# The first group of outputs moved up behind the last group of scores, in a fused perceiver kernel on one core

## The chip, the cores and the metric

The kernel runs on one core of one Trainium2 chip. The metric is the device time of one execution in microseconds. A core has five engines that run side by side: TensorE (matrix products, PE in the profile), VectorE (DVE), ScalarE (ACT), GpSimd (POOL) and SyncE (SP), whose queue issues transfers here. They wait for one another by semaphores, and each engine works through its own list of instructions in the order written.

## The reference

The input x is (4, 256, 256): four batches, 256 tokens, 256 features; a context is (4, 4096, 256). Three parts are added to x one after another: a masked cross attention to the context, a linear attention, and a stack of six layers of local attention and feed-forward. The change lies in the third part:

```python
def local_attention(q, k, v):      # 16 heads of 64, windows of 64 tokens
    sim = jnp.einsum('bhwie,bhwje->bhwij', bq, bk2) * QK_SCALE
    sim = jnp.where(mask, -jnp.finfo(sim.dtype).max, sim)
    attn = jax.nn.softmax(sim, -1)
    out = jnp.einsum('bhwij,bhwje->bhwie', attn, bv2)

def attn_layer(x, Wqkv, qs, ksc, Wo):
    qkv = x @ Wqkv                  # 256 -> 3 * 1024
    q = l2norm(q) * qs              # and k; then a rotation with a scale
    out = local_attention(q, k, v)
    return out @ Wo

for i in range(6):
    x = attn_layer(shift_tokens(x), ...) + x
    x = ffn_layer(shift_tokens(x), ...) + x
```

A token attends to the tokens of its own window of 64 and of the one before. `shift_tokens` takes half of the features from the token before.

## The kernel before

The kernel runs four stages in turn; only the third, `local_layers` (line 1363 on), is of interest here. Its order of work is written out by hand, one function per engine, and the order within each engine is fixed by the calls.

**Slots.** The stage works in slots, one batch of one layer each: 6 layers of 4 batches are 24 slots. In a slot, TensorE (`slot`, line 1659) does the attention of batch b, the projections to queries, keys and values of the next batch (`ahead`; not in the very last slot), and the feed-forward of the batch before (`ffn`; not in the first). Layers 1 to 4 are a loop on each engine; layers 0 and 5 stand outside it. The input of the batch two slots on is turned as well (`turn`).

**TensorE's units.** `turn_qk` turns queries and keys (16 heads, in 8 groups through PSUM). `scores(a, g)` computes the scores of 4 heads (two pairs) as 32 matmuls in tiles of 64 by 64. `turn_probs(a, pair)` turns the probabilities of one pair with 4 matmuls into the one bank TURN. `out(a, L, b, g)` multiplies the turned probabilities of two pairs with the values, as 24 matmuls in tiles of 128 by 64, into the bank OUT. `project(n, nb, j)`, j from 0 to 11, is one unit of 6 matmuls with 512 columns, for a split of each number into a high and a low part; units 0 to 7 give queries and keys, 8 to 11 values. They alternate between two banks, so unit j waits until unit j - 2 has been copied out. `turn_xn`, `widen` (six) and `narrow` are the feed-forward, `project_out` the attention's last product.

**What stands around them.** ScalarE (`slot`, line 1821) copies each projection out (`qkv_out`, line 1765), takes the exponentials of a pair (`exps`, four instructions, line 1786), copies turned probabilities out (`probs_out`, line 1793) and some outputs (`o_out`, line 1800). Its order around the change is: exps 4, exps 5, qkv_out 7, qkv_out 8, probs_out 2, exps 6, qkv_out 9, o_out 0, qkv_out 10, probs_out 3, qkv_out 11, and then xn_out. The buffer `pT` has two halves, so probs_out 2 overwrites what the first group of outputs reads, and waits for it; the conditions are in these lines:

```python
def probs_out(a, pair):
    act.wait_ge(o_full, a + 4 * (pair // 2))
    act.wait_ge(pT_full, a + 2 * pair + 2)
def out(a, L, b, g):
    pe.wait_ge(pT_done, a + 4 * (g + 1))
    pe.wait_ge(o_done, a + 4 * g)
```

VectorE (`slot`, line 2106) adds the band mask, scales and takes the minima of a pair (`minima`, line 2023), divides by the totals (`share`, line 2039), rotates and normalises queries and keys, and does the gated products of the feed-forward (`gated`, line 2089).

**Weights.** In the third slot of each layer (b = 2) but the last layer, SyncE's queue loads the next layer's query and key weights (`load_layer_weights`, line 180) as four transfers of 512 KB. It waits for the eighth projection, unit 7, of that slot:

```python
sp.wait_ge(qkv_full, L + U * 3 + 8)
k.load_layer_weights(sp, i + 1, "qk")
```

ScalarE rounds them in twelve pieces (`weights_high`, line 1754) through that slot. The first piece stands right behind `xn_out` and ahead of probs_out 4, the input's copy (`x_out`), exps 7, probs_out 5, the second piece and the first gate (`gates`, line 1818). The queue's next entries are the values' small transfers (`middle`, lines 1479 and 1480), which wait for the last projection.

Of the kernel before, what the change touches and what calls it, by code (L numbers as in the profile page):

```python
# [116 lines left out]
def hold(eng, sem):  # L117

    eng.sem_inc(sem, 1)
# [1243 lines left out]
def local_layers(k):  # L1363
# [8 lines left out]
    with ExitStack() as ctx:  # L1372
# [48 lines left out]
        def score_at(pair, e, t):  # L1421

            bank, col = (2 if pair // 2 % 2 else 4) + e, (pair % 2) * T + t * P
            return bank, slice(col, col + P)
# [90 lines left out]
        def _(pe):  # L1515
# [10 lines left out]
            def project(a, b, j):  # L1526

                if j == 0:
                    pe.wait_ge(xT_done, a + U)
                    pe.wait_ge(u_done, a - 2 * U)  # L1530
                if b == 0 and (j < 4 or j in (8, 9)):
                    pe.wait_ge(w_low, a + after_piece(2 * (j if j < 4 else j - 4) + 1))
                t, part = divmod(j, 4) if j < 8 else divmod(j - 8, 2)
                col = part * 512 if j < 8 else 2 * INNER + part * 512
                if j >= 2:
                    pe.wait_ge(qkv_done, a + j - 1)
                for kk in range(KD):
                    for n, (px, pw) in enumerate(PARTS):
                        ins = pe.matmul(ps[:, DENSE + j % 2, :], xT[:, px, kk, t * P:(t + 1) * P], wqkv[pw][:, kk, col:col + 512],  # L1539
                                        start=kk == 0 and n == 0, stop=kk == KD - 1 and n == 2)  # L1540
                ins.then_inc(qkv_full, 1 if j < SLOTS - 1 else U - SLOTS + 1)

            def turn_qk(a):
                pe.wait_ge(rope_done, a + U)
                pe.wait_ge(q_rope_done, a + U)
                pe.wait_ge(s_read, a)
                for g in range(8):
                    two, s = divmod(g, 2)
                    if g == 2:
                        pe.wait_ge(y_mid, a)  # L1550
                    if g == 3:
                        pe.wait_ge(y_out, a - U + LAYER)
                    if g >= 4:
                        pe.wait_ge(k_done if s else q_done, a + 4 * (two - 1))
                    for i in range(2):
                        for t in range(TT):
                            col = s * INNER + (2 * two + i) * P
                            ins = pe.transpose(ps[:, TURN_QK[g % 4], i * T + t * P:i * T + (t + 1) * P],  # L1558
                                               qk[:, t, col:col + P], k.ident)
                    ins.then_inc(qk_full, 2)  # L1560

            def scores(a, g):

                if g < 2:
                    pe.wait_ge(q_done, a + 4 * (g + 3))
                    pe.wait_ge(k_done, a + 4 * (g + 3))
                else:
                    pe.wait_ge(s_read, a + 4 * (g - 1))
                hold(pe, pe_held)
                for pair in (2 * g, 2 * g + 1):  # L1570
                    for t in range(TT):
                        for n in range(2):
                            w = 2 * t + n
                            k0 = max(w - 1, 0) * WINDOW
                            for e in range(2):
                                head = slice(e * DH, (e + 1) * DH)
                                bank, cols = score_at(pair, e, t)
                                ins = pe.matmul(ps[n * WINDOW:(n + 1) * WINDOW, bank, cols],  # L1578
                                                qT[head, pair, w * WINDOW:(w + 1) * WINDOW], kT[head, pair, k0:k0 + P],
                                                start=True, stop=True)  # L1580
                ins.then_inc(s_full, 4)

            def turn_probs(a, pair):
                pe.wait_ge(p_done, a + 2 * pair + 2)
                pe.wait_ge(pT_done, a + 2 * pair)
                for i in range(2):
                    for t in range(TT):
                        at = (i * TT + t) * P
                        ins = pe.transpose(ps[:, TURN, at:at + P], prob[:, 2 * (pair % RING) + i, t, :], k.ident)  # L1589
                ins.then_inc(pT_full, 2)  # L1590
# [5 lines that stand above are left out]
                if g == 0:  # L1596
                    pe.wait_ge(qkv_done, a + U)
                    pe.wait_ge(mid_in[b % 2], L + 32 * (b // 2 + 1))
                for pair in (2 * g, 2 * g + 1):
                    at = (pair % 2) * T  # L1600
                    for values, t, q0, q1 in ((v[:, b % 2, 0, :], 0, 0, P), (v_mid[:, b % 2, :], 1, 0, WINDOW),
                                              (v[:, b % 2, 1, :], 1, WINDOW, P)):
                        for i in range(2):
                            col = (2 * pair + i) * DH
                            ins = pe.matmul(ps[i * DH:(i + 1) * DH, OUT, at + t * P + q0:at + t * P + q1],  # L1605
                                            values[:, col:col + DH], pT[:, pair % 2, i, t, q0:q1], start=True, stop=True)
                ins.then_inc(o_full, 4)
# [12 lines left out]
            def turn_xn(a, ahead):  # L1620
                pe.wait_ge(xn_done, a + U)
                if ahead:
                    pe.wait_ge(qkv_done, a + 2 * U + SLOTS - 1)
                pe.wait_ge(u_done, a)
                for kk in range(KD):
                    for t in range(TT):
                        ins = pe.transpose(ps[:, DENSE, kk * T + t * P:kk * T + (t + 1) * P],  # L1627
                                           xn[:, t, kk * P:(kk + 1) * P], k.ident)
                ins.then_inc(xnT_full, U)
# [29 lines left out]
            def slot(L, b, ffn, ahead, turn):  # L1659

                a = L + U * b
                f, fb = L + U * (b - 1), (b - 1) % B
                n, nb = L + U * (b + 1), (b + 1) % B
                turn_qk(a)
                scores(a, 0)
                if ahead:
                    project(n, nb, 0)
                scores(a, 1)
                if ahead:
                    project(n, nb, 1)  # L1670
                    project(n, nb, 2)
                turn_probs(a, 0)
                if ahead:
                    project(n, nb, 3)
                    project(n, nb, 4)
                scores(a, 2)
                turn_probs(a, 1)
                if ahead:
                    project(n, nb, 5)
                    project(n, nb, 6)  # L1680
                scores(a, 3)
                turn_probs(a, 2)
                if ahead:
                    project(n, nb, 7)
                    project(n, nb, 8)
                out(a, L, b, 0)
                if ahead:
                    project(n, nb, 9)
                    project(n, nb, 10)
                turn_probs(a, 3)  # L1690
                if ahead:
                    project(n, nb, 11)
                if ffn:
                    turn_xn(f, ahead)
                out(a, L, b, 1)
                turn_probs(a, 4)
                if turn:
                    turn_x(L + U * (b + 2), (b + 2) % B)
                if ffn:
                    widen(f, fb, 0, turn)  # L1700
                turn_probs(a, 5)
                if ffn:
                    widen(f, fb, 1, turn)
                out(a, L, b, 2)
                turn_probs(a, 6)
                if ffn:
                    widen(f, fb, 2, turn)
                turn_probs(a, 7)
                if ffn:
                    widen(f, fb, 3, turn)  # L1710
                out(a, L, b, 3)
                if ffn:
                    widen(f, fb, 4, turn)
                    widen(f, fb, 5, turn)
                project_out(a, b)
                if ffn:
                    narrow(f, fb)
# [640 lines left out]
```

## Time and profile before

| | |
|---|---|
| device time, median of 3 runs | 2299.36 us (2296.36 to 2299.97) |
| the profiled execution's own time | 2297.52 us |
| its span | 2295.7 us |
| TensorE matmul busy | 2117.8 us, 92% of the span, 16354 instructions |
| VectorE busy | 1706.1 us, 74% |
| ScalarE busy | 1337.3 us, 58% |
| GpSimd busy | 494.0 us, 22% |
| mean granted clock of TensorE | 0.971 of full speed |
| chain that ended last, by engine | PE 54%, issue 2%, ACT 2%, DVE 1%, DMA 1% |

The local stage runs from about 907 us to the end. The span is from the first to the last instruction that the profiler records. In a row of the timeline the columns are start, duration (both in us), engine, line of the kernel, operation, output and inputs, shapes and a count; in brackets stands how long the engine was idle before it and what ended that. Matmuls overlap, so the time of a unit is read from its start to the start of the next.

### The profile page before, as it was taken

Reading aid. Unit: us, or ns where it says so; the run is one execution under the profiler, and the core shown is the slowest. Engines: PE = TensorE matmul, PEld = TensorE weight load, DVE = VectorE, ACT = ScalarE, POOL = GpSimd, SP = SyncE. Lnnn points to the kernel's source line nnn. Section 1 sums busy time; section 2 is a strip of 40 time slices with the busy share of each in tenths; the row PEclk is TensorE's granted clock in tenths of the full one; section 3 lists DMA queues with packets and bytes.
Section 4 is the critical chain, followed back from the end, with each engine's and each line's share of the span. In section 5 each row is a group of like instructions: output and inputs, shape, how many; then the busy total and the mean of one; then the engine's idle time right before and its main releaser. Section 6 shows DMA issues by size and latency. Waiting matters only on the chain.

```text
span 2295.7 us, 49701 instructions
## 1 busy us (share of the span) xinstructions
PE 2117.8 (92%) x16354; PEld 1715.7 (75%) x16354; DVE 1706.1 (74%) x4834; ACT 1337.3 (58%) x3908; POOL 494.0 (22%) x274
## 2 busy tenths in 40 slices
PE   3899999999998665899999999999999999999986
PEld 3677777777776444788888888888888888888875
DVE  5777577567564466789888978897889788988872
ACT  1667556556554004567666766676667666766651
POOL 2111111111110002223222322232223222322210
PEclk9999999999999787899999999999999999999998
DMA  3000000000000400002110211021102110111000
GB/s 112 7 10 1 6 11 1 6 11 1 6 24 1 147 0 10 13 13 68 31 49 13 68 33 49 13 68 33 49 13 67 33 49 18 62 31 49 13 13 21
DMA packets 47107, 70.12 MB, mean 31 GB/s; under 512 B 9078, under 2 KB 33828, under 8 KB 46628
## 3 DMA queue, kind: packets, MB, share of 16 engines
q1 hardware_dynamic: 44516, 62.34, 8.8%
q10 hardware_dynamic: 2368, 4.98, 0.6%
q8 instruction: 119, 1.95, 0.3%
q14 instruction: 104, 0.85, 0.1%
HBM read 50.54 MB, written 1.05 MB: 22 GB/s over the span
## 4 chain that ended last, share of the span: by engine, by line
PE 54%; issue 2%; ACT 2%; DVE 1%; DMA 1%; POOL 0%; SPq 0%; DVEq 0%; ACTq 0%; POOLq 0%
PE ps_loc L1539 17%; PE ps_loc L1645 10%; PE ps_loc L1616 7%; PE ps_loc L1655 5%; PE ps_loc L1578 4%; PE ps_loc L1589 4%; PE ps_loc L1605 4%; PE ps_loc L1558 3%; DMA late<-y_all 1%; ACT prob_loc L1786 0%; PE ps_loc L1627 0%; DMA w_raw<-in_ffn_Wqkv_dram 0%; PE ps_loc L1522 0%; ACT L1818 0%; POOL rnorm L2269 0%
## 5 line engine op out<-in xcount | busy, mean ns | idle before, releaser
L2269 POOL TENSOR_TENSOR rnorm<-norm_floor,half_loc 128x32 f32<-128x32 f32 x48 | 302.4, 6300 | 621.2 <-DVE norm_floor L1959 499.1
L1539 PE MATMUL ps_loc<-w_high,xT 128*128 128x512 f32 x1152 | 379.1, 410 | 5.4 <-DVE w_low L1948 3.8
L1786 ACT ACTIVATE prob_loc<-prob_loc,top_loc 128x128 f32<-128x128 f32 x768 | 298.5, 398 | 40.1 <-DVE top_loc L2023 37.3
L1645 PE MATMUL ps_loc<-xnT_loc,w 128*128 128x256 f32 (+1 forms) x1056 | 252.7, 385 | 2.4 <-DVE kT_loc L2089 1.2
L644 ACT ACTIVATE prob<-prob,new_top 128x256 f32<-128x256 f32 x512 | 252.1, 496 | 0.0
L1539 PEld LDWEIGHTS ps_loc<-w_high,xT 128*128 128x128 f32 x1152 | 204.7, 189 | 55.7 <-issue 11.8
L820 DVE CUSTOM_DVE_ANT_0 prob<-ps_cross,bias 128x256 f32<-128x256 f32 x512 | 186.2, 420 | 71.2 <-PE ps_cross L435 57.6
L2023 DVE CUSTOM_DVE_ANT_0 prob_loc<-ps_loc,const,rnorm 128x128 f32<-128x128 f32 x768 | 218.6, 344 | 27.2 <-PE ps_loc L1578 25.5
L1778 ACT ACTIVATE qT_loc<-ps_loc 128x512 f32<-128x512 f32 x96 | 57.3, 597 | 301.2 <-PE ps_loc L1558 301.2
L1539 PE MATMUL ps_loc<-w_low,xT 128*128 128x512 f32 x576 | 228.4, 397 | 0.0
L1645 PEld LDWEIGHTS ps_loc<-xnT_loc,w 128*128 128x128 f32 (+1 forms) x1056 | 191.4, 190 | 28.9 <-DVE kT_loc L2089 2.4
L1616 PE MATMUL ps_loc<-wo,qT_loc 128*128 128x256 f32 x768 | 171.8, 382 | 0.8 <-ACT qT_loc L1800 0.8
L1616 PEld LDWEIGHTS ps_loc<-wo,qT_loc 128*128 128x128 f32 x768 | 147.3, 192 | 21.8 <-issue 1.0
L1015 POOL TENSOR_TENSOR o<-o,alpha 128x1024 f32<-128x1024 f32 x32 | 60.9, 1904 | 455.2 <-DVE o L859 350.7
L1786 ACT ACTIVATION_READ_ACCUMULATOR prob_loc<-prob_loc,top_loc 128x1 f32 x768 | 150.4, 196 | 0.0
L458 PE MATMUL ps_cross<-const,prob 128*128 128x128 f32 x1024 | 141.5, 282 | 6.7 <-ACT probT L652 4.0
L458 PEld LDWEIGHTS ps_cross<-const,prob 128*128 128x128 f32 x1024 | 111.0, 141 | 45.8 <-issue 30.6
L1793 ACT ACTIVATE pT<-ps_loc 128x512 f32<-128x512 f32 x192 | 113.9, 593 | 49.6 <-PE ps_loc L1589 37.8
L2039 DVE TENSOR_TENSOR prob_loc<-prob_loc,total_loc 128x512 f32<-128x512 f32 x192 | 132.5, 690 | 2.7
L435 PE MATMUL ps_cross<-kT,qT 64*128 64x256 f32 x1024 | 129.3, 391 | 5.5 <-DVE chunk_top L820 4.2
L1589 PE MATMUL ps_loc<-const,prob_loc 128*128 128x128 f32 x768 | 122.3, 282 | 10.5 <-DVE prob_loc L2039 8.1
L1655 PE MATMUL ps_loc<-w,kT_loc 128*128 128x256 f32 x576 | 128.3, 379 | 1.2 <-DVE kT_loc L2089 1.2
(184 smaller groups left out, 4265.8 us busy)
## 6 DMA issues: line engine op xcount, KB each, us to landing
w_raw<-in_ffn_Wqkv_dram SPq DMA_DIRECT2D x24, 512.0 KB, 5.4
v_mid<-v_loc SPq DMA_DIRECT2D x48, 256.0 KB, 3.6
w_raw<-in_ffn_Wqkv_dram SPq DMA_DIRECT2D x24, 256.0 KB, 4.0
wo<-in_ffn_Wo_dram SPq DMA_DIRECT2D x24, 256.0 KB, 3.6
w<-in_ffn_W_dram SPq DMA_DIRECT2D x12, 341.0 KB, 3.9
w<-in_ffn_W_dram SPq DMA_DIRECT2D x6, 640.0 KB, 4.8
ctx_raw<-in_ctx_dram SPq DMA_DIRECT2D x12, 256.0 KB, 2.6
w<-in_ffn_W_dram SPq DMA_DIRECT2D x12, 256.0 KB
```

Of the source, the lines that this page charges most:

```text
L458: ins = pe.transpose(ps[:, TURN + t, (i * TT + lt) * P:(i * TT + lt + 1) * P], prob[:, lt, 2 * pair + i, t * P:(t + 1) * P], k.ident)
L644: ins = act.activation(prob[:, t, h, :], prob[:, t, h, :], ACT.Exp, bias=new_top[:, t, h:h + 1], scale=-1.0, accum_out=chunk_sum[:, t, h:h ...
L820: ins = dve.tensor_tensor_reduce(out=prob[:, t, h, :], in0=ps[:, banks[pair % 2] + i, t * CHUNK:(t + 1) * CHUNK], in1=key_bias, scale=1.0, ...
L1539: ins = pe.matmul(ps[:, DENSE + j % 2, :], xT[:, px, kk, t * P:(t + 1) * P], wqkv[pw][:, kk, col:col + 512], start=kk == 0 and n == 0, sto ...
L1589: ins = pe.transpose(ps[:, TURN, at:at + P], prob[:, 2 * (pair % RING) + i, t, :], k.ident)
L1616: ins = pe.matmul(ps[:, WIDE_OUT, t * D:(t + 1) * D], oT[:, pair, t * P:(t + 1) * P], wo[:, pair, :], start=pair == 0, stop=pair == PAIRS - 1)
L1645: ins = pe.matmul(ps[0:n, DENSE + m % 2, part * T:(part + 1) * T], w1[:, kk, col:col + n], xnT[:, kk, :], start=kk == 0, stop=kk == KD - 1)
L1655: ins = pe.matmul(ps[:, FFN_OUT, t * D:(t + 1) * D], uT[:, m, t * P:(t + 1) * P], w2[:, m, :], start=m == 0, stop=m == FM - 1)
L1786: ins = act.activation(pr, pr, ACT.Exp, bias=top[:, h, t:t + 1], scale=-1.0, accum_out=total[:, h, t:t + 1])
L2023: ins = dve.tensor_tensor_reduce(out=prob[:, 2 * (pair % RING) + e, t, :], in0=ps[:, bank, cols], in1=band, scale=rnorm[:, b % 2, t, h:h + ...
L2039: dve.tensor_tensor(pr, pr, by, ALU.mult).then_inc(p_done, 2)
L2269: pool.tensor_tensor(rnorm[:, b % 2, t, :], norm2_floor[:, :], half[:, :], ALU.pow).then_inc(rnorm_done, 8)
```

## The change

The call of the first group of outputs, `out(a, L, b, 0)`, moves on TensorE from behind the projections 7 and 8 to directly behind the last group of scores, ahead of `turn_probs(a, 2)` and of these two projections. The four projections 7 to 10 then follow one another. No other engine's order is touched.

```diff
@@ -1679,12 +1679,11 @@
                     project(n, nb, 5)
                     project(n, nb, 6)
                 scores(a, 3)
+                out(a, L, b, 0)
                 turn_probs(a, 2)
                 if ahead:
                     project(n, nb, 7)
                     project(n, nb, 8)
-                out(a, L, b, 0)
-                if ahead:
                     project(n, nb, 9)
                     project(n, nb, 10)
                 turn_probs(a, 3)
```

## Rows read from the trace of the kernel before

**Rows 1.** Busy time in one slot: stretch and length, then each engine (instructions), clock, DMA.

```profile
1132.23:1188.30 56.07, 56.05 (x469) 46.83 (x468) 46.45 (x123) 36.75 (x104) 14.84 (x4) 1.00 0.11 32
```

**Rows 2.** Timeline of that slot, TensorE, from the last scores on.

```profile
1150.23 1.10 PE L1578 MATMUL ps_loc<-kT_loc,qT_loc 64*64 64x128 f32 x32
1151.27 0.66 PE L1589 MATMUL ps_loc<-const,prob_loc 128*128 128x128 f32 x4
1151.68 0.71 PE L1539 MATMUL ps_loc<-w_high,xT 128*128 128x512 f32 x2
...
1153.16 0.63 PE L1539 MATMUL ps_loc<-w_high,xT 128*128 128x512 f32 x2
...
1154.65 0.44 PE L1605 MATMUL ps_loc<-pT,v_loc 128*64 128x128 f32 x4
...
1155.71 0.73 PE L1539 MATMUL ps_loc<-w_high,xT 128*128 128x512 f32 x2
...
1157.21 0.63 PE L1539 MATMUL ps_loc<-w_high,xT 128*128 128x512 f32 x2
...
1158.61 0.60 PE L1589 MATMUL ps_loc<-const,prob_loc 128*128 128x128 f32 x4
1158.96 0.71 PE L1539 MATMUL ps_loc<-w_high,xT 128*128 128x512 f32 x2
...
1160.44 0.60 PE L1627 MATMUL ps_loc<-const,xn_loc 128*128 128x128 f32 x4
```

**Rows 3.** Timeline of the same stretch, ScalarE.

```profile
1154.76 0.60 ACT L1765 ACTIVATE v_loc<-ps_loc 128x512 f32<-128x512 f32 x1
1155.87 0.60 ACT L1793 ACTIVATE pT<-ps_loc 128x512 f32<-128x512 f32 x1 [0.51 <-PE ps_loc L1605]
1156.59 0.40 ACT L1786 ACTIVATE prob_loc<-prob_loc,top_loc 128x128 f32<-128x128 f32 x1
...
1158.15 0.58 ACT L1765 ACTIVATE v_loc<-ps_loc 128x512 f32<-128x512 f32 x1
...
1160.70 0.60 ACT L1765 ACTIVATE v_loc<-ps_loc 128x512 f32<-128x512 f32 x1 [0.52 <-PE ps_loc L1539]
1161.19 1.02 ACT L1809 ACTIVATE xnT_loc<-ps_loc,vec 128x256 f32<-128x256 f32 x2
```

**Rows 4.** The same stretch, VectorE: the last step of the pair's minima.

```profile
1156.21 0.34 DVE L2023 CUSTOM_DVE_ANT_0 prob_loc<-ps_loc,const,rnorm 128x128 f32<-128x128 f32 x1
```

**Rows 5.** Timeline of the third slot, ScalarE.

```profile
1043.41 0.41 ACT L1786 ACTIVATE prob_loc<-prob_loc,top_loc 128x128 f32<-128x128 f32 x1 [0.34 <-DVE top_loc L2023]
...
1044.97 0.58 ACT L1765 ACTIVATE v_loc<-ps_loc 128x512 f32<-128x512 f32 x1
```

**Rows 6.** Timeline of the third slot, TensorE.

```profile
1045.60 0.73 PE L1539 MATMUL ps_loc<-w_high,xT 128*128 128x512 f32 x2
...
1047.12 0.38 PE L1627 MATMUL ps_loc<-const,xn_loc 128*128 128x128 f32 x2
```

**Rows 7.** The chain that ended last, third slot: start, length, what.

```profile
1041.31 7.68 DMA w_raw<-in_ffn_Wqkv_dram
...
1049.01 0.41 ACT w_high L1754
```

**Rows 8.** The weight load of slot 7: durations in ns, first and last start.

```profile
L180 SPq DMA_DIRECT2D w_raw<-in_ffn_Wqkv_dram x4: 333/336/356, 1265.8 to 1267.4; - x4
...
DMA to landing us min/median/max: 3.9/5.1/6.2
```

**Rows 9.** Timeline of slot 7, ScalarE: its first weight rounding.

```profile
1274.33 0.64 ACT L1754 ACTIVATE w_high<-w_raw 128x512 fp32r<-128x512 f32 x1
```

**Rows 10.** Timeline of the last slot, TensorE: the turns of pairs 2 and 3.

```profile
2225.77 0.66 PE L1589 MATMUL ps_loc<-const,prob_loc 128*128 128x128 f32 x4 [1.58 <-DVE prob_loc L2039]
...
2228.67 0.63 PE L1589 MATMUL ps_loc<-const,prob_loc 128*128 128x128 f32 x4 [1.20 <-ACT pT L1793]
```

**Rows 11.** Waits from 906 to 2209 us: who, for what, us in total, times, longest.

```profile
ACT qT_loc L1778 <- PE ps_loc L1558: 288.3, 92, 12.4
```

## The prediction

> **What bounds the kernel now.** I began with the busy time of one slot of the local stage. A slot is one batch of one layer; there are 24, and 23 of them also carry the projections of the next batch. In the slot of [rows 1] TensorE is busy 56.05 of 56.07 us, at full clock, so only its own work and its rare waits count there. The page's chain agrees: it runs over TensorE nearly everywhere. Next I read TensorE in order of time through the part that is edited [rows 2], then ScalarE over the same stretch [rows 3] and the one VectorE step that gates it [rows 4]. I use these names for the units of work: S3 is the last scores, O0 the first outputs, T2 and T3 are turns of probabilities, P7 to P11 projections, N the turn of the normalised input. [Rows 2] give S3 at 1150.23, T2 1151.27, P7 1151.68, P8 1153.16, O0 1154.65, P9 1155.71, P10 1157.21, T3 1158.61, P11 1158.96, N 1160.44: no idle. S3 to N is 10.21 us, and the other 22 slots with projections repeat it within 0.1.
>
> ScalarE is less loaded but comes close. Its copy of P9 starts at 1158.15 and lasts 0.58, so it ends at 1158.73 [rows 3]; P11 cannot start without it and starts at 1158.96. The margin is 0.23 us. In the third slot there is none: there the copy of P9 starts at 1044.97 and ends at 1045.55 [rows 5], and P11 starts at 1045.60 [rows 6], 0.05 after it.
>
> **The change, part by part.** Nothing is added or taken away in work; O0 goes ahead of T2, P7 and P8. Four things follow.
>
> (1) **TensorE's own time shrinks.** From [rows 2]: S3 lasts 1.04, O0 1.06, T2 behind a group in small tiles 0.41, the projection behind a turn 1.48, one between projections 1.40 (P10 to T3), T3 0.35. P8 takes 1.49 because O0 follows, P9 takes 1.50 because O0 is ahead of it. The new order would run O0 1151.27, T2 1152.33, P7 1152.74, P8 1154.22, P9 1155.62, P10 1157.02, T3 1158.42, P11 1158.77 at the earliest: 0.19 sooner. The one junction that no row shows is S3 to O0. S3 has 1.04 ahead of T2, and I take the same ahead of O0. Its bounds: no cheaper, since S3's matmuls are the same; at most 0.10 dearer, which is what P8 pays ahead of O0 (1.49 against 1.40).
> The Trainium skill (TensorEngine Tiling (Array Packing), Key Properties) says that a change of tiling mode drains the engine. By that rule the stretch has four changes now and three afterwards, and leaving S3 costs the same whatever follows. The extra 0.09 and 0.10 in P8 and P9 agree with it; taken alone, the rule would promise the 0.19 in every slot.
>
> (2) **ScalarE takes it back.** Its order is fixed: copy of P8, probabilities out of T2 (p2), four exponentials (e6), copy of P9. Now p2 waits for O0, because it overwrites the buffer that O0 reads: the row at 1155.87 has 0.51 of idle put down to O0, and the copy of P8 was done during O0, from 1154.76 [rows 3]. With O0 early, that wait is gone, but P8 ends where O0 ended, and its copy now stands ahead of p2. A copy after a long wait starts 0.26 after the next unit's start (N 1160.44 in [rows 2], copy 1160.70 in [rows 3]); after a short one about 0.20 (0.11 behind O0's start, plus the 0.09 by which P8 is lengthened). So the copy starts at 1155.82 to 1155.88, p2 0.49 later (1160.70 to 1161.19), e6 0.47 to 0.49 after that: 1156.78 to 1156.86, in place of 1156.59. Until now e6 waited for the minima, whose last step runs from 1156.21 for 0.34 [rows 4]; this cover is what is used up. In the third slot e6 starts at 1043.41 [rows 5] and N at 1047.12 [rows 6], 3.71 later, with P11 waiting in between. So here N comes at 1160.49 to 1160.57 against 1160.44: 0.05 to 0.13 late. I take 0.09, the middle, per slot. TensorE gains 0.19 and then waits about 0.28 ahead of P11.
>
> (3) **A transfer passes behind it on SP's queue.** The load of the next layer's query and key weights waits for P7 of the third slot of each of five layers, and P7 ends 1.06 later. ScalarE's first weight rounding waits for that load, and behind it on ScalarE are probabilities out, the next input, exponentials, and the first gate, on which a widening on TensorE waits. In the third slot the chain shows this: the transfer runs 7.68 us from 1041.31, to 1048.99, and the rounding starts at 1049.01 [rows 7]. That slot gains no cover, so 1.06 is added. Inside the loop the issues run from 1265.8 to 1267.4 and the slowest takes 6.2 to landing [rows 8]: about 1273.6, with the rounding at 1274.33 [rows 9] because ScalarE is busy until then. Add 1.06: 1274.66, 0.35 late by these rounded rows; I take 0.3, since it need not be the last that is the slowest. It replaces the 0.09 there and doesn't add to it. Bounds: 0.09 where it stays hidden, 1.06 where it was bound before.
>
> (4) **What costs nothing.** O0's own conditions are older than S3 (p1's buffer, and the values, copied in the slot before). T2 only gets later than its share. P9 needs the copy of P7, done by about 1155.1, and P10 that of P8, done by 1156.5 against 1157.02: cover 0.5. N needs the copy of P10, and the second outputs need p3; both move by about 0.2, with 0.5 and more in hand. GpSimd and the small transfers of values wait for none of the moved units. The last slot has no projections: T2 there waits 1.58 for VectorE's share and T3 1.20 for ScalarE's copy [rows 10]; O0 merely fills the first wait, T3's own condition doesn't move, so nothing is won. No shift is caught up between slots: ScalarE waits for the next slot's first turns 92 times, 288 us in all [rows 11], so it starts each slot from TensorE's time.
>
> **The sum.** 23 slots less the five with weights is 18: 18 x 0.09 = 1.6. Four slots in the loop: 4 x 0.3 = 1.2. The third slot: 1.06. Together +3.9 us on the profiled execution's 2297.5 (its span of 2295.7 and 1.8 around it, which the change doesn't touch), which gives 2301.4. That execution lies 1.8 under the median of 2299.4, so the forecast is **2303.2 us**, or +0.17%. A measurement of this kernel can tell about 0.2% from no change, here 4.6 us.
>
> **The rivals.**
> A, *the weight load decides, slower*. The transfer of the third slot took 7.68, that in the loop 6.2. If the loop's are as slow as that, 1.5 is added to 1273.6 + 1.06, and each rounding is some 1.8 late: 4 x 1.8 + 1.06 + 1.6 = 9.9. If only half of that comes, about 6, or 2305.5. It decides from 0.16 us more per weight slot ((4.6 - 3.9) / 5). For it: a transfer already ended the wait once. Against: the rows in the loop left 0.7 us over. Chance 0.16.
> B, *ScalarE keeps up, TensorE's gain stays*. 18 x -0.19 = -3.4; the weight slots still give 2.3: -1.1, 2298.3. Only with the weights hidden as well would it be 23 x -0.19 = -4.4, 2295.0. For it: the idle of 0.51 ahead of p2 is removed. Against: ScalarE's chain from P9's new start to P11 is at least 0.20 + 0.49 + 0.47 + 1.56 (1156.59 to 1158.15 in [rows 3]) + 0.58 + 0.05 = 3.35 us, where TensorE's own way is 3.15. Chance 0.08. This is the case that the skill's rule on tiling changes alone would give.
> C, *leaving the scores straight into the outputs costs more*. With 0.10 on S3, P7 and P8 and all behind them are later: 23 x 0.10 = 2.3, together 6.2, 2305.5, slower by 0.27%. Chance 0.14.
> D, *the early outputs change nothing*, because ScalarE needs only what it needed: 0 to +1, 2299.4 to 2300.4. Chance 0.12.
>
> **How the numbers follow.** The forecast keeps 0.50. B and D are mostly within 0.2%, with 0.03 of B beyond on the fast side; A and C are slower, but the upper part of my forecast's own bounds (0.13 for 0.09, 0.5 for 0.3: +5.4) is too, and part of A and C isn't. So faster 0.03, within 0.2% 0.67, slower 0.30. The lower end, 2299.6, takes in D and leaves out most of B; the upper, 2306.8, takes in C and half of A. No more than 2 in 10 is outside.
>
> **What the changed profile would show.** S3 to O0 at 1.03 to 1.04; P8, P9 and P10 at 1.40 each; P11 waiting for ScalarE's copy of P9 by 0.2 to 0.3 in nearly all of 23 slots; S3 to N at 10.26 to 10.34; no more idle of ScalarE ahead of p2 put down to the outputs; the last weight transfer landing a microsecond later against its slot, and the first rounding starting right at it in five slots, with the wait of the third widening longer there. I am wrong if P11 starts without a wait, if S3 ahead of O0 takes over 1.08, or if the rounding of the weight slots doesn't move.

## The result and the profile after

The changed kernel takes 2303.14 us in the median of 11 runs (2300.16 to 2307.66), the kernel before, in 11 runs beside it, 2297.56 (2292.32 to 2301.06). The ratio is 1.0025, with a 95% interval of 1.0016 to 1.0035: slower by a quarter of a per cent, 5.6 us. The forecast was 2303.2 us, +0.17%. The profiled execution of the changed kernel took 2305.2 us with a span of 2303.3, against 2297.5 and 2295.7 before.

I read the changed part first in the slot that answers to [rows 1] to [rows 4]. Timeline of TensorE, changed kernel, from the last scores on:

```profile
1149.87 1.10 PE L1578 MATMUL ps_loc<-kT_loc,qT_loc 64*64 64x128 f32 x32
1150.90 0.44 PE L1605 MATMUL ps_loc<-pT,v_loc 128*64 128x128 f32 x4
...
1151.96 0.66 PE L1589 MATMUL ps_loc<-const,prob_loc 128*128 128x128 f32 x4
1152.37 0.72 PE L1539 MATMUL ps_loc<-w_high,xT 128*128 128x512 f32 x2
...
1153.85 0.63 PE L1539 MATMUL ps_loc<-w_high,xT 128*128 128x512 f32 x2
...
1155.25 0.63 PE L1539 MATMUL ps_loc<-w_high,xT 128*128 128x512 f32 x2
...
1156.65 0.63 PE L1539 MATMUL ps_loc<-w_high,xT 128*128 128x512 f32 x2
...
1158.05 0.60 PE L1589 MATMUL ps_loc<-const,prob_loc 128*128 128x128 f32 x4
1158.60 0.73 PE L1539 MATMUL ps_loc<-w_high,xT 128*128 128x512 f32 x2
...
1160.10 0.60 PE L1627 MATMUL ps_loc<-const,xn_loc 128*128 128x128 f32 x4
```

The last scores (S3) take 1.03 us ahead of the outputs (O0), and projections 8 to 10 take 1.40 each: 1153.85, 1155.25, 1156.65, 1158.05. The turn of pair 3 (T3) comes at 8.18 us after S3, in place of 8.38. But T3 to projection 11 (P11) is now 0.55 in place of 0.35, and the turn of the input (N) comes 10.23 us after S3, in place of 10.21. The gain of 0.2 is there and is given back ahead of P11. All 23 slots with projections look like this, with 10.23 in the loop and 10.29 outside it; in the first slot, which has no N, outputs follow P11, and they start 10.38 us after S3.

ScalarE over the same stretch (p2 is its copy of the turned probabilities of pair 2, e6 the exponentials of pair 6):

```profile
1155.45 0.60 ACT L1764 ACTIVATE v_loc<-ps_loc 128x512 f32<-128x512 f32 x1 [0.80 <-PE ps_loc L1539]
1155.94 0.59 ACT L1792 ACTIVATE pT<-ps_loc 128x512 f32<-128x512 f32 x1
1156.42 0.40 ACT L1785 ACTIVATE prob_loc<-prob_loc,top_loc 128x128 f32<-128x128 f32 x1
...
1157.96 0.58 ACT L1764 ACTIVATE v_loc<-ps_loc 128x512 f32<-128x512 f32 x1
```

The copy of projection 8 starts 0.20 us after projection 9, p2 0.49 later, e6 0.48 later, and the copy of projection 9 ends at 1158.54; P11 starts at 1158.60, 0.06 behind it.

Where the time goes is in the third slots of the loop's layers, those that load weights. Busy time by slot, the kernel before (columns as in [rows 1]):

```profile
1244.48:1301.03 56.55, 56.30 (x469) 46.86 (x468) 50.40 (x130) 42.84 (x116) 18.90 (x9) 1.00 0.21 68
1472.36:1528.92 56.56, 56.31 (x470) 46.86 (x468) 50.40 (x130) 42.86 (x116) 18.92 (x9) 1.00 0.21 68
```

The changed kernel, the first row the slot of [rows 1], the others the two above:

```profile
1131.87:1187.96 56.09, 56.06 (x469) 46.95 (x468) 46.47 (x123) 36.66 (x104) 14.83 (x4) 1.00 0.11 32
...
1244.16:1301.88 57.72, 56.67 (x469) 46.92 (x468) 50.60 (x130) 42.71 (x116) 18.90 (x9) 1.00 0.20 67
1473.06:1531.02 57.96, 56.78 (x469) 46.91 (x468) 50.62 (x130) 42.70 (x116) 18.91 (x9) 1.00 0.21 67
```

An ordinary slot is longer by 0.02, these two by 1.17 and 1.40, and the other two in the loop by 1.30 and 1.04: 4.9 us in four slots. The chain of the changed kernel (start, length, what) runs through the weight load in the first of them:

```profile
1268.09 7.30 DMA w_raw<-in_ffn_Wqkv_dram
1275.39 0.02 issue
1275.42 0.04 ACT w_high L1753
```

The waits of ScalarE over the loop (who, for what, us in total, times, longest) have a row that the kernel before has not:

```profile
ACT w_high L1753 <- DMA w_raw<-in_ffn_Wqkv_dram: 5.3, 4, 1.5
```

TensorE first feels it one widening earlier than the prediction had it, in the second one, which waits for the low part of the next input (timeline, TensorE; 0.62 us of idle):

```profile
1277.92 1.99 PE L1645 MATMUL ps_loc<-xnT_loc,w 128*128 128x256 f32 x8 [0.62 <-DVE xT L1941]
```

The spans of the two profiled executions differ by 7.6 us. From the starts of the slots: the stages ahead of the local one +1.2, the first slot -1.7, the four weight slots +4.9, the other 18 slots up to the last +0.8, the last slot and the feed-forward behind it +2.4. The stages ahead of the local one hold the same code; over all fourteen profiles they end between 900.4 and 908.3 us. The figures for the first and the last slot go with TensorE's granted clock. In the first slot it was half in one stretch before, and full there after the change (busy time, the kernel before, then the changed one):

```profile
942.00:956.00 14.00, 10.59 (x67) 8.71 (x68) 11.36 (x13) 3.97 (x5) 2.79 (x1) 0.51 0.00 1
942.00:956.00 14.00, 9.13 (x84) 7.65 (x82) 12.18 (x15) 5.14 (x12) 3.24 (x1) 1.00 0.06 18
```

This goes with the order. The first slot took 52.3 us in all seven profiles that have the early outputs in it and ScalarE's order of before (the changed kernel, e1, e3 and e9 to e12 below), and 53.8 to 54.1 in the other seven. So some 1.7 us of gain belong to the change. The clock falls 35 us into the slot in the others, for some 13.7 us, and only at its end in the seven; why isn't shown.

From 2200 to 2240 us the granted clock was 0.96 before and 0.88 after. From the start of the last slot to the end it took 86.8 us before and 89.2 after; the same seven profiles have 89.2 to 90.8, but of the four with the old order in that slot e4 and e7 have 89.4 and 89.3, and only e2 has 86.9. Whether the order has a part in it is open, and it is left out of the account.

### The profile page after: what moved, and what is told of

Read it like the earlier page. It is cut to its first block, busy times and chain, and to the rows that moved or that the text cites. A ratio compares the mean times of both kernels' runs of the same rounds, so it can differ in the third digit from the quotient of the medians.

```text
span 2303.3 us, 49701 instructions
## 1 busy us (share of the span) xinstructions
PE 2122.1 (92%) x16354; PEld 1719.9 (75%) x16354; DVE 1707.3 (74%) x4834; ACT 1335.2 (58%) x3908; POOL 494.0 (21%) x274
## 4 chain that ended last, share of the span: by engine, by line
PE 53%; ACT 2%; DMA 2%; issue 2%; DVE 1%; POOL 0%; SPq 0%; DVEq 0%; ACTq 0%; POOLq 0%
PE ps_loc L1539 16%; PE ps_loc L1645 10%; PE ps_loc L1616 7%; PE ps_loc L1655 5%; PE ps_loc L1578 4%; PE ps_loc L1605 4%; PE ps_loc L1589 4%; PE ps_loc L1558 3%; DMA w_raw<-in_ffn_Wqkv_dram 1%; ACT prob_loc L1785 1%; PE ps_loc L1627 0%; DMA late<-y_all 0%; PE ps_loc L1522 0%; ACT pT L1792 0%; ACT L1817 0%
```

## The experiments

Theory W: the later issue of the weight load carries the loss. Theory A: ScalarE's chain behind the copy of projection 8 takes TensorE's gain back. The rival R to W: the loss lies in the order itself and is spread over all slots.

**e1, old place in the third slots only.** The call stays behind the projections 7 and 8 where b is 2.

```diff
-                out(a, L, b, 0)
+                if b != 2:
+                    out(a, L, b, 0)
                 turn_probs(a, 2)
...
+                if not (b != 2):
+                    out(a, L, b, 0)
```

> The outputs stay in their old place in the third slot of each layer (the one that loads weights) and are early in the other 19. Theory W (the weight load carries the loss): only 0.03 to 0.09 us in each of 18 slots is left, +0.5 to +1.6 us or +0.02 to +0.07% against the kernel before, that is no difference. Rival R (the new order itself costs, in every slot or by its instruction layout): most of the +0.25% stays, at least +0.15%. The third slots should be back at 56.55 us each in the loop.

Measured: 2297.87 us, ratio 1.0003 (0.9993 to 1.0013). The third slot that stood at 57.72 is back:

```profile
1240.36:1296.93 56.57, 56.31 (x470) 46.85 (x469) 50.41 (x130) 42.92 (x116) 18.90 (x9) 1.00 0.21 68
```

**e2, new place in the third slots only.** The same edit with `b == 2`. This holds for six slots; the last layer's third slot loads no weights.

> The complement: the outputs are early only in the third slot of each layer. Theory W: nearly the whole loss, four slots in the loop with +1.0 to +1.4 us each and the one outside between 0 and +1, together +4.5 to +6 us, +0.20 to +0.26%. Rival R (a loss spread over all slots): a quarter of it, +0.06%.

Measured: 2304.81 us, ratio 1.0029 (1.0017 to 1.0041), all of the loss, and a little more than the 0.26% expected at most. Here the load is late in all five third slots that have one (waits of ScalarE):

```profile
ACT w_high L1757 <- DMA w_raw<-in_ffn_Wqkv_dram: 7.1, 5, 1.8
```

These five slots are longer than before by 0.98 to 1.69 us, 6.6 in all; the last layer's third slot by 0.09. Five of 24 slots carry the loss; R falls with these two runs.

**e3, the load split.** The new order throughout. The first half of the columns is used last by unit 5, so its two transfers needn't wait for unit 7.

```diff
-                    sp.wait_ge(qkv_full, L + U * 3 + 8)
-                    k.load_layer_weights(sp, i + 1, "qk")
+                    for j, units in ((0, 6), (1, 8)):
+                        sp.wait_ge(qkv_full, L + U * 3 + units)
+                        k.load_layer_weights(sp, i + 1, "qk", (j,))
```

> The new order everywhere, but the load of the query and key weights is split: the two transfers for the columns of units 0, 1, 4 and 5 are issued after unit 5, the other two after unit 7 as before. Theory W: the last landing comes a microsecond or more earlier, the first weight rounding no longer waits for it, and the kernel is back within 0.1% of the one before (+0.5 to +1.6 us). Rival R: still +0.2% or more. If the transfers are as late as now although half was issued earlier (a collision that holds one engine, whatever the load), the slots with weights keep part of their +1.2 us.

Measured: 2299.33 us, ratio 1.0009 (1.0000 to 1.0017). ScalarE's wait for the load is gone, and the third slot is at 56.59:

```profile
1242.73:1299.32 56.59, 56.34 (x469) 46.97 (x468) 50.45 (x130) 42.76 (x116) 18.91 (x9) 1.00 0.22 68
```

What is left, +0.09%, is of the size of theory A's 0.03 to 0.09 in each slot (1 to 2 us).

**e4, the split load on the order before.** The control to e3.

> Control for the split load: the order of the kernel before with the load of the query and key weights split as in e3. In the loop the load already landed 0.8 us ahead of its use, so nothing is won there; outside it the third slot may win up to 1 us. Expected -0.5 to 0 us, within 0.05%.

Measured: 2298.66 us, ratio 1.0006 (0.9994 to 1.0018). The split gains nothing where the load is covered. It gained nothing in the third slot outside the loop either (56.71 us, 56.72 before), where up to 1 us seemed possible.

**e7, the order before with a later load.** One line: the load waits for unit 8.

```diff
-                    sp.wait_ge(qkv_full, L + U * 3 + 8)
+                    sp.wait_ge(qkv_full, L + U * 3 + 9)
```

> The order of the kernel before, untouched, but the weight load waits for unit 8 in place of unit 7, so it is issued about 1.5 us later (1.06 in the change). Theory W: 0.7 us of cover, so at least +0.8 us in each of the four slots in the loop, and more, 1.7 us, if the transfers are also slowed as in the change; the third slot 0 to +1.5: together +4 to +8 us, +0.17 to +0.35%. Rival R: nothing, within 0.05%.

Measured: 2302.54 us, ratio 1.0025 (1.0014 to 1.0036). A late load alone costs as much as the change does. Its profiled execution took 2298.17 us, 4.4 less than that median. In its loop the load was issued 0.35 us later against its slot than in the change, and yet ScalarE waited little:

```profile
ACT w_high L1754 <- DMA w_raw<-in_ffn_Wqkv_dram: 1.7, 3, 0.8
```

The four slots there are longer than before by 0.03 to 0.73 us, where at least 0.8 was expected. So the length of the load varies as well, which I hadn't expected: from the last issue to the last landing it took 5.8 to 6.5 us in this profile's loop slots, 7.2 to 7.5 in the change's. The loss stands outside the loop, in the third slot, which took 56.72 us before:

```profile
1012.52:1072.40 59.88, 58.19 (x470) 47.96 (x469) 50.72 (x130) 42.71 (x116) 18.88 (x10) 0.97 0.20 65
1048.40:1051.80 3.40, 3.40 (x26) 2.52 (x26) 2.35 (x5) 2.54 (x4) 0.00 (x0) 0.50 0.04 13
```

Its load took 8.56 us (chain that ended last), ScalarE waited 2.4 us for it and TensorE 1.7 behind that, and then TensorE's granted clock was half for 3.4 us, the second row:

```profile
1036.41 8.56 DMA w_raw<-in_ffn_Wqkv_dram
```

From the start of the first slot to that of the last this execution is 4.7 us longer than the one before. Its total hides that, because its stages ahead of the local one, which the edit doesn't touch, took 6.5 us less.

**e5, probabilities first on ScalarE.** New order; p2 goes ahead of the copies of projections 7 and 8.

```diff
                 exps(a, 5)
+                probs_out(a, 2)
                 if ahead:
                     qkv_out(n, nb, 7)
                     qkv_out(n, nb, 8)
-                probs_out(a, 2)
                 exps(a, 6)
```

> The new order on TensorE, and on ScalarE the copy of the turned probabilities of pair 2 goes ahead of the copies of projections 7 and 8. Theory A (ScalarE's chain behind the copy of projection 8 holds projection 11): the exponentials of pair 6 start at the minima's end again (6.36 us after the last scores, 6.55 to 6.61 in the change), the wait ahead of projection 11 shrinks from 0.20 to 0.26 us to under 0.06, and the last scores to the turn of the input takes 10.05 to 10.08 us in place of 10.23 to 10.29; against the change 18 slots x 0.18 = -3.2 us (the slots with weights stay held by the load), that is about +2 us or +0.1% against before. Rival: the wait has another cause (the bank, the turn of pair 3): it stays, and the time is that of the change, +0.25%.

Measured: 2300.07 us, ratio 1.0010 (0.9998 to 1.0022). TensorE in the slot that answers to [rows 2], which starts at 1129.79 here:

```profile
1147.80 1.10 PE L1578 MATMUL ps_loc<-kT_loc,qT_loc 64*64 64x128 f32 x32
...
1155.98 0.60 PE L1589 MATMUL ps_loc<-const,prob_loc 128*128 128x128 f32 x4
1156.35 0.73 PE L1539 MATMUL ps_loc<-w_high,xT 128*128 128x512 f32 x2
...
1157.85 0.60 PE L1627 MATMUL ps_loc<-const,xn_loc 128*128 128x128 f32 x4
```

T3 to P11 is 0.37, S3 to N 10.05. On ScalarE, e6 is gated by the minima again:

```profile
1154.16 0.40 ACT L1785 ACTIVATE prob_loc<-prob_loc,top_loc 128x128 f32<-128x128 f32 x1 [0.19 <-DVE top_loc L2022]
```

Theory A stands: the same TensorE order, with a ScalarE order that fits it, keeps most of the gain. The total is 1.8 us under that of e9 below, less than the 3.2 expected; the first slot is back at 53.8 us, with 13.7 us of it at half clock.

**e6 and e13, both repairs.** New order, split load, probabilities first.

> Both repairs together on the new order. If both theories hold, the wait ahead of projection 11 is gone and the weight load hidden: 23 slots x -0.15 = -3.4 us against before, -0.15%; if the weight slots keep 0.3 us, -2.5 us. If either theory is wrong, no better than the kernel before.

Measured: 2295.29 us, ratio 0.9994 (0.9984 to 1.0004). Third slot and ordinary slot, against 56.55 and 56.07 before:

```profile
1241.54:1297.95 56.41, 56.16 (x470) 46.97 (x469) 50.39 (x130) 42.75 (x116) 18.90 (x9) 1.00 0.21 68
1129.59:1185.52 55.93, 55.90 (x470) 46.95 (x469) 46.45 (x123) 36.65 (x104) 14.83 (x4) 1.00 0.11 32
```

> e6 once more, since its first interval (0.9984 to 1.0004 of the time before) holds both no difference and the -0.15% that its profile adds up to (23 slots x -0.15 us). If the profile's account is right, 0.998 to 0.9995 again.

Measured again: 2295.86 us, ratio 0.9997 (0.9988 to 1.0006). The profiles show 0.14 us per slot, some 3 us in all, but neither the 0.15% expected of e6 nor the 0.05% or more expected of e13 came, and the runs can't tell what came from nothing. It is faster than the changed kernel (the intervals of e6 and of e9 below don't meet), not measurably faster than the one before.

**e9 and e12, the changed kernel again; e10 and e11, padded.** These ask why the load takes 7.3 us in the change and 6.2 before. In the five microseconds behind the last issue, the changed kernel's slot 7 has a second kind of transfer (transfers by queue in that stretch):

```profile
q1 hardware_dynamic: 508, 1.89, 95.7%
q8 instruction: 1, 0.02, 1.2%
```

The kernel before has none in that slot:

```profile
q1 hardware_dynamic: 526, 1.93, 97.6%
```

It is a piece of program, one packet of 16 KB, which takes 0.95 us. Theory F: such a piece lengthens a load that it falls into. Its rival V: the values' transfers that follow do.

> The changed kernel once more, on the same chip as e4 to e6, for direct comparison: +0.25% against before, and in its profile again a first weight rounding that waits 1.0 to 1.5 us for the transfer in the third slots of the loop.

Measured (e9): 2301.85 us, ratio 1.0016 (1.0007 to 1.0026), less than the 0.25% expected. In its profile the rounding started late by 1.7, 2.0, 0.6 and 0.8 us against the kernel before in the four slots of the loop, and ScalarE waited 1.55, 1.84, 0.46 and 0.64, none of them the 1.0 to 1.5 expected; the last two are the ones without a program piece in the load.

e10 and e11 put idle semaphore increments ahead of the last scores where b is 2:

```diff
+                if b == 2:
+                    for _ in range(40):
+                        hold(pe, pe_held)
                 scores(a, 3)
```

> The changed kernel with 40 more semaphore increments on TensorE's queue ahead of the last scores, in the third slots only; they shift where its program is fetched in 16 KB pieces. The time itself says little (the increments cost TensorE something). Theory F (the weight load is slow when such an instruction transfer falls among its packets): in each third slot, last weight transfer from issue to last landing 7.0 us or more where a 16 KB instruction transfer starts between 23.4 and 29.7 us of the slot, and under 6.8 us where none does; with 40 more instructions it should move from about 25.6 to a place ahead of the load in some or all of them. Rival V (the load collides with the values' transfers that follow it, because it is issued later): 7.0 us or more in all of them, wherever the instruction transfer is.

> The same with 80 increments. Theory F: the same rule by the place of the instruction transfer, which moves further. Rival V: 7.0 us or more in all third slots of the loop.

> The changed kernel once more, one look: how often the slow load comes. Theory F: 7.0 us or more in just those third slots of the loop in which an instruction transfer starts between 23.4 and 29.7 us; in two profiles so far that was 6 of 8.

Measured: e10 2335.49 us, e11 2375.13, e12 2306.41, one run each. In e12, slot 7 had no program piece in its load and slot 11 had one; the durations of their loads, first slot 7:

```profile
DMA to landing us min/median/max: 3.7/5.1/6.5
```

and slot 11:

```profile
DMA to landing us min/median/max: 4.2/5.4/7.9
```

Here is the whole count over the unsplit loads, from the last issue to the last landing, by when the 16 KB piece starts behind the last issue:

| profiles | piece 1.4 to 4.7 us behind | loads, us | elsewhere or none | loads, us |
|---|---|---|---|---|
| before | 1 | 7.68 | 4 | 6.07 to 6.39 |
| change, e9, e12 | 9 | 7.18 to 7.89 | 6 | 6.13 to 6.70 |
| e10, e11 | 0 | | 10 | 5.96 to 6.79 |
| e1, e2, e5, e7 | 9 | 6.99 to 8.56 | 11 | 5.81 to 6.79, one 7.83 |

F's rule holds in 49 of 50 loads in this form. But the stretch of 1.4 to 4.7 us was drawn from these same loads. The one that was expected, 23.4 to 29.7 us of the slot, fits worse: pieces from 29.1 on (5.1 us and more behind the last issue) do no harm, and in e10 and e11 the padding delays the load itself by 6 to 13 us, so that in nine of their ten slots a piece starts within that stretch, well ahead of the load, and the load is short.

V falls: in e10 and e11 the values' transfers follow as in the change (5.2 us behind the last issue in the loop, 5.6 outside), and all ten loads are under 6.8 us; in e7 they follow sooner (4.8 us in the loop), and four of five loads are short.

Two more counts bear F out. A load has 64 landings, 16 for each of its transfers, and in a slow load only the last of them is late: in slot 7 the 63rd and 64th came 5.89 and 6.16 us behind the last issue in the kernel before, 6.21 and 7.30 in the changed one. Over all 50 loads the 63rd came at 5.96 to 6.99 us in the 20 of 6.99 us and more, at 5.79 to 6.63 in the other 30. And of the split loads of e3, e6 and e13 the second half took 5.60 to 5.94 us in the eight cases with a piece 2.5 to 3.4 us behind the last issue, 4.36 to 4.66 in the other seven. That one of the 16 engines is held up by the piece fits this, but the traces don't name the engine of a packet, so this last step is argued and not shown.

The one load of 7.83 (in e2, its piece 2.8 us ahead of the last issue) stays open. So does why the same program's pieces come at 20.5 us of the slot in one execution and at 28.6 in the next.

## Why the prediction was right or wrong

The number came out almost exactly, 2303.14 us for 2303.2, and that is luck. The forecast stood on 2299.4 us for the kernel before, which measured 2297.6 beside the change, 1.8 less; and the increase was 5.6 us for 3.9, 1.7 more. The ratio, +0.25% for +0.17%, tells more: some terms were too small and others too large.

*TensorE's own time (1): right.* Every start of the new order came within 0.02 us of the listed ones, counted from S3. The one junction no row had shown, S3 to O0, took 1.03 to 1.04. Rival C is out. The Trainium skill's rule (TensorEngine Tiling (Array Packing), Key Properties: a change of tiling mode drains the engine) agrees with the rows: S3 costs the same whether the next unit is a whole-array turn or outputs in another tiling, and P8 and P9 lost their extra 0.09 and 0.10.

*ScalarE's chain (2): the mechanism right, its size twice too large.* N moved by 0.02 to 0.09 us where 0.05 to 0.13 was expected; inside the loop ScalarE started 0.20 behind the next unit, the lower end of my bounds, and N there came only 0.03 late, less than that end allows; outside the loop it started 0.26 behind. I took 0.09 for all; 1.6 us was forecast for 18 slots, about 0.8 measured. e5 shows the cause: with p2 moved, the wait ahead of P11 shrinks from 0.20 to about 0.02 in most slots. Rivals B and D are out with it.

*The weight load (3): the mechanism right, its size wrong.* This is the term that failed: "four slots in the loop: 4 x 0.3 = 1.2". They cost 4.9 (6.6 with the third slot in e2). The issue did come 1.06 later, but I kept the load's length at the 6.2 of [rows 8], while it grew to 7.2 to 7.5. [Rows 7] held the warning: the same load at 7.68 in the third slot. I used it only for that slot, and as the price of rival A, with a chance of 0.16. Rival A's own price, 1.8 late at each rounding, 9.9 in all, was too high (the roundings came 1.28 to 1.65 late), its half was about right. Its threshold is off in the sum: (4.6 - 3.9) / 5 is 0.14 us per weight slot, not 0.16; no chance changes with it. By e1, e2, e3 and e7 this term is the loss.

*The third slot: wrong by 1.06 the other way.* It took 56.72 before and after. Its load was slow before, with a program piece 3.9 us behind the last issue, and normal after (6.13, its piece 5.6 us behind); the 1.06 of later issue was met by a load shorter by 1.5, so the rounding came 0.24 earlier instead of 1.06 later. In e2, where this load was slow again (7.66), the slot took 57.73, the 1.06 or so of the forecast: the term hung on where a program piece fell.

*What costs nothing (4): right in what was named, with two omissions.* GpSimd, the last slot's turns and the values' transfers moved nothing. The clock wasn't thought of: the first slot gained some 1.7 us by it in every profile with this order and ScalarE's order of before. Nor was it thought of that the program itself arrives by transfers, which would be shifted against the load. In the weight slots the second widening also waited, 0.62 in slot 7, ahead of the third one that I named; both hang on the same rounding.

The chances leaned to "within 0.2%" with 0.67, for a measured 0.25%, whose interval reaches from 0.16 to 0.35%.

## What to carry to other kernels

When a unit moves past another on one engine, look at each transfer that waits for the unit that is pushed back: here 1 us of later issue in five slots cost more than the 0.2 us in each of 23 slots that the order could have won. Read such a transfer's length in every place where it occurs, not in one; its slowest case is the one that a thinner cover will show. Here the better order on the busiest engine was kept only once the engine that empties its banks had its order changed with it. And before an absolute number is called a hit, look whether the kernel before still measures what the forecast stood on.

## What the runs showed of the hardware

A 16 KB piece of program that starts 1.4 to 4.7 us behind the last issue of a 2 MB weight load (four transfers of 512 KB) goes with a load of 6.99 to 8.56 us; otherwise it is 5.81 to 6.79, but for one case in 31. Of the load's 64 landings only the last is late.

Forty semaphore increments on TensorE's queue left its array idle for 4.23 us, eighty for 10.23 (e10 and e11, third slot of the last layer): 0.15 us for each of the further forty. The granted clock was then 0.50 for 6.8 and 10.2 us there, so that the slot grew by 6.4 and 12.4.

With the outputs early and ScalarE's order of before, the first slot ran at full clock from 4 us after its start to its end in seven of seven profiles; in the other seven it was at half clock for some 13.7 us more (granted clock 0.51 from 942 to 956 us in the kernel before).

Leaving 64 by 64 tiles costs the same towards 128 by 64 tiles as towards the whole array, 1.03 to 1.04 us for the 32 matmuls.
